# A shifted loop end and idle matrix products in TensorE's waits, in a four-layer convolution network

## The reference, cut to what matters

```python
x = x + _L0_conv_ref(_gn(x), w_real, w_imag, b_real, b_imag)   # 3x3 convolution in the Fourier plane, complex weights
x = x + _L1_conv_ref(_gn(x))                                   # gates: sign of a row's product with the sum of the other half
x = x + _L2_conv_ref(_gn(x), W)                                # 3x3 convolution
x = x + _L3_conv_ref(_gn(x), weight)                           # 3x3 convolution
return x
```

## Time and profile before

| what | value |
|---|---|
| median of 3 runs | 4733.0 us (4728.77 to 9641.31) |
| profiled execution | 4716.25 us |
| its span | 4714.5 us |
| granted TensorE clock, mean over the span | 0.959 |
| busy: TensorE, VectorE, ScalarE | 4226.5, 3331.8, 2541.0 us |

### The profile page before, as it was taken

The page is one execution under the profiler, slowest core; times in us unless marked ns, Lnnn a source line. Parts: engine busy times, 40 slices in busy tenths (PEclk is TensorE's granted clock), DMA queues, the critical chain, the costliest instruction groups (busy, mean ns, idle before and its releaser), DMA issues.

```text
span 4714.5 us, 229091 instructions
## 1 busy us (share of the span) xinstructions
PE 4226.5 (90%) x84848; PEld 2660.6 (56%) x84848; DVE 3331.8 (71%) x13348; ACT 2541.0 (54%) x8637; POOL 1.0 (0%) x6
## 2 busy tenths in 40 slices
PE   4898989989899898998989989899898999988799
PEld 1455765556555566555655556555665556655476
DVE  1887658876588665887658876588756887578873
ACT  4675526655267542775437754377533675335552
POOL 0000000000000000000000000000000000000000
PEclk8999999989999899999999999999999998999999
DMA  7442015520156202661026610356003560034304
GB/s 190 128 136 77 4 40 179 186 82 4 43 184 188 73 4 56 185 187 60 3 66 189 187 46 3 87 184 189 28 3 104 181 185 18 3 99 140 96 4 146
DMA packets 290241, 467.98 MB, mean 99 GB/s; under 512 B 25536, under 2 KB 92288, under 8 KB 289408
## 3 DMA queue, kind: packets, MB, share of 16 engines
q1 hardware_dynamic: 289536, 457.92, 32.2%
HBM read 323.60 MB, written 134.22 MB: 97 GB/s over the span
## 4 chain that ended last, share of the span: by engine, by line
PE 60%; DVE 12%; DMA 8%; issue 8%; SPq 5%; ACT 3%; DVEq 1%; ACTq 1%
PE ps L1352 35%; PE ps L1255 9%; DMA raw<-x 8%; PE ps L1270 4%; PE ps L1263 3%; PE ps L1279 3%; PE ps L1125 2%; DVE shared L858 2%; SPq L426 2%; SPq L433 1%; DVE xin L853 1%; DVE shared L854 1%; ACT x L584 1%; SPq L407 1%; DVE shared L860 1%
## 5 line engine op out<-in xcount | busy, mean ns | idle before, releaser
L1352 PE MATMUL ps<-x,conv_s 32*32 32x512 f32 x49104 | 1753.1, 608 | 76.2 <-DVE x L1016 41.0
L1352 PEld LDWEIGHTS ps<-x,conv_s 32*32 32x32 f32 x49104 | 1246.7, 104 | 520.0 <-issue 290.2
L1255 PE MATMUL ps<-shared 32*32 32x512 f32 x16384 | 654.0, 603 | 0.0
L662 ACT ACTIVATE x<-ps,vec 128x256 f32<-128x256 f32 x512 | 214.6, 470 | 738.6 <-PE ps L1352 738.6
L1270 PEld LDWEIGHTS ps<-hil,shared 128*128 128x128 f32 x4096 | 500.3, 193 | 194.1 <-issue 193.3
L584 ACT ACTIVATE x<-ps,vec 128x128 f32 (+1 forms) x1024 | 376.7, 384 | 430.2 <-PE ps L1270 429.1
L858 DVE SCALAR_TENSOR_TENSOR shared<-xin,trig 128x128 f32<-128x128 f32 x2048 | 530.9, 299 | 106.6 <-DVE shared L854 98.8
L1279 PE MATMUL ps<-eye,vsb 128*128 128x128 f32 x2048 | 369.0, 303 | 222.5 <-DVE vsb L879 127.5
L1270 PE MATMUL ps<-hil,shared 128*128 128x128 f32 x4096 | 567.5, 282 | 0.0
L1086 DVE SCALAR_TENSOR_TENSOR x<-ps,x 128x256 f32<-128x256 f32 x512 | 214.9, 420 | 423.2 <-ACT x L662 422.3
L1255 PEld LDWEIGHTS ps<-shared 32*32 32x32 f32 x16384 | 306.9, 103 | 280.7 <-issue 217.1
(11 more groups left out here) (202 smaller groups left out, 4641.5 us busy)
## 6 DMA issues: line engine op xcount, KB each, us to landing
out<-x SPq DMA_DIRECT2D x512, 256.0 KB
shared<-x SPq DMA_DIRECT2D x448, 256.0 KB
raw<-x SPq DMA_DIRECT2D x256, 256.0 KB
raw<-x SPq DMA_DIRECT2D x512, 128.0 KB
shared<-t_strip SPq DMA_DIRECT2D x512, 96.0 KB, 4.0
x<-x SPq DMA_DIRECT2D x64, 256.0 KB, 7.9
x<-t_proj SPq DMA_DIRECT2D x1, 2048.0 KB, 13.3
trig<-t_trig SPq DMA_DIRECT2D x1, 512.0 KB, 9.9
```

What stands on the lines that cost most here:

```text
L1255: mm = pe.matmul(ps[TM * cg:TM * cg + TM, bank, :], wst[TM * rg:TM * rg + TM, k, v, a, :], of[TM * rg:TM * rg + TM, :], start=(a == AXS), ...
L1352: mm = pe.matmul(halves(ps[TM * cg:TM * cg + TM, banks[k], :]), conv_s[TM * rg:TM * rg + TM, kw, second, :], x1b[TM * rg:TM * rg + TM, of, ...
```

## The change

On TensorE the statistics behind layer 0 become a function of their own, `first_statistics`, and the loop's body is now convolutions of image i, the first layer of image i + 1 and the first statistics of image i + 1; so the branch stands between `prepare_h` and layer 2. A new function `keep_clock(count)` writes count products of the identity (128 by 128 weights) with 512 columns of a table into bank 2, from which nothing is read before it is written anew. Three stand behind `prepare_z`, three behind `prepare_h`, three behind layer 2 (with a wait of their own, for the eviction of the pair that held bank 2) and two behind the third statistics. In the last image there is no `prepare_z` and no `prepare_h`, but the products stand there too. No other engine's code is changed. Nothing in the output depends on the new products.

```diff
-            def convolutions(i, more):
+            def keep_clock(count):
+
+                for _ in range(count):
+                    pe.matmul(ps[:, BY + 2, :], eye[:], trig[:, 0, :], start=True, stop=True)
+
+            def first_statistics(i, more):
 
                 pe.wait_ge(v_part, i + 1)
                 pe.matmul(ps[:, BH, 0:2], partner[:], vec[:, EPS_Q:EPS_Q + 2], start=True, stop=True).then_inc(p_part, 1)
...
                 if more:
                     prepare_z(i + 1)
+                keep_clock(3)
 
                 pe.wait_ge(v_sums2, i + 1)
                 statistics(G_OUT, vec[:, ST:ST + 2], stat[:, 0:2], gsel, P).then_inc(p_stat2, 1)
                 if more:
                     prepare_h(i + 1)
+                keep_clock(3)
+
+            def convolutions(i, more):
 
                 def taps(n, p, banks, outputs, second, kw, done=None):
...
+                pe.wait_ge(evicted, ev(i, 1 + STRIPS - 2 * DEPTH2 + 4))
+                due()
+                keep_clock(3)
                 pe.wait_ge(v_sums3, i * 2 + 2)
                 statistics(G_OUT, vec[:, ST:ST + 2], stat[:, 0:2], gsel, P).then_inc(p_stat3, 1)
+                keep_clock(2)
                 pe.wait_ge(v_conv3, i + 1)
...
             first_layer(0, True)
+            first_statistics(0, True)
             with pe.Fori(0, B - 2) as i:
                 convolutions(i, True)
                 first_layer(i + 1, True)
+                first_statistics(i + 1, True)
             convolutions(B - 2, True)
             first_layer(B - 1, False)
+            first_statistics(B - 1, False)
             convolutions(B - 1, False)
```

## The result

The changed kernel takes 4703.97 us in the median of 17 runs (4688.93 to 4716.78), against 4733.55 us for the kernel before, measured beside it. The ratio is 0.9934, with a 95% interval from 0.9922 to 0.9946: about 30 us faster, as forecast. By parts the fit is looser, as the traces show.

The account below looks back on a forecast made before the run. TensorE, busy 90% of the span, was taken to lose time at the loop's branch and to half clock after idling. Terms −14.2 + 3.5 − 8 − 5 − 6 gave about −30 us, from 4733.0 to 4703 us; range 4670 to 4733.

Parts of the forecast that it names:

- The loop's end: Branch between layer 0 and the partner product: moving it behind prepare_h takes 14.2 us off the path.
- The first group: Three idle products before the second statistics: they delay these by 0.5 us in seven images, +3.5 us in all.
- The second group: Three idle products behind prepare_h: they give back 8 of 30.8 us lost to the clock at layer 2's start.
- Between layer 2 and layer 3: Idle products in the two waits there: faster one-column products save 5 us, bounds 0 and 9.6.
- The start of layer 3: First 6 us of layer 3: a third of the 17.5 us lost to the clock comes back, 6 us.
- the mean clock of layer 2's starts: Sign of being right: granted clock of layer 2's first 14 us above 0.75 on average.
- the hidden branch: Sign of being right: before layer 2, a sequencer branch of 4.6 us that ends before VectorE's gates.
- the 15.5 to 17: Sign of being right: 15.5 to 17 us from layer 0's last product to layer 2 in all images.
- The loop's end alone: Rival: the clock drops all the same and only the moved branch counts, 4725 us; chance 0.24, uncovered branch included.
- the clock held everywhere: Rival: full clock at all starts and one-column products, −72 us, 4661 us; chance 0.14.
- the slower case: Rival: idle products at half clock outlast the waits and become the new wait, +49 us, 4782 us; chance 0.07.
- The uncovered branch: Rival: the moved branch gains nothing before layer 2's dense taps, costing up to 8.5 us; counted within the 0.24.

Follow-up runs that it names:

- the two filled kernels: Two, six, three and three idle products, with the moved loop end (4670.5 us, ratio 0.9855) and with the loop's end where it was (4676.42 us, 0.9886).
- thin: The changed kernel with idle products of one column instead of 512; 4723.74 us, ratio 0.9965 to the kernel before.
- first_only: The changed kernel with only the three products before the second statistics, other groups and the eviction wait removed; 4713.49 us, ratio 0.9963 to before.
- filled: The changed kernel with two, six, three and three idle products instead of three, three, three and two; 4670.5 us, ratio 0.9855 to before.
- loop_only: The changed kernel without any idle products or the wait for evictions, only the moved loop end; 4725.84 us, ratio 0.9989 to before.

## Why the prediction was right, and where only its sum was

*The loop's end (−14.2 us).* Its place on the path was right: 14.9 us less in the stretch with the loop's end alone, 14.0 between the two filled kernels, no "issue" in front of layer 2, and the branch hidden. In whole runs it measured 5 us alone (0.9989, up to 14 by the interval), 17 and 18 in the two other kernels that have the moved end and whose products leave layer 2 starting at half clock (`thin`, `first_only`), and 15 with the filled waits. So 14.2 fits, but how much of it arrives in whole runs is not settled closer than that.

*The first group (+3.5).* 128.7 and 129.2 us stand against 124.2 with the loop's end alone, so +4.5 to +5, and +5.8 where it stands alone. The term fell short by 1 to 2 us; image 0 alone bore 2.2 us (17.8 in place of 15.6), where I had put 0.5 on each image. What I did not see is its second price: the clock that it raises shortens the second group, and opens the idling in which the clock falls.

*The second group (−8).* I named the 2.8 us left idle and took a quarter of the loss as recovered. From before to after the loss fell from 30.8 and 39.7 us to 19.3 and 18.4, and layer 2 as a whole became 16 us shorter (means of two traces each, 877.1 to 861.2). But two traces of one kernel differ there by 9 us. The six traces without full-width products behind `prepare_h` lost 18.9 to 39.2 us, 29.9 in the mean; the three with three in front and three behind lost 20.4 in the mean. By that the second group brought 9.5 us (layer 2 was 9 us shorter), so the term was of the right size or too small by up to 8; the traces can't tell.

*Between layer 2 and layer 3 (−5).* Too small: 82.1 us became 74.6 and 73.7, −8. The one-column stretches took 27.8 us in all before, and 19.0 and 17.9 after. The bias products ran wholly at full clock in three and in four of the eight images (1.4 us) and partly at half in the others (up to 2.1); the first of the one-column products follows 1.3 to 1.5 us of idling. I had kept 5 of 9.6. Over more traces the stretch is 82.8 us in the mean without full-width products in it and 73.1 with three and two, −10.

*The start of layer 3 (−6).* Too large for the changed kernel: 17.5 and 18.8 us lost became 17.1 and 15.1, next to nothing, and layer 3 did not get shorter (984.6 and 988.4 to 988.2 and 985.8). Over more traces it comes nearer: five without full-width products between the layers lost 19.1 us in the mean there, six with three and two 13.7, and their layer 3 was 3.3 us shorter. The prediction had warned that the clock may be down again behind the one-column stretch. With three products in the second wait the loss is 4.9 to 7.9 us.

So by the two kernels' own traces the parts are −10 − 16 − 8 + 0 = −34, and by the means over more traces −10 − 9 − 10 − 3 = −32; the runs say −30. That the sum came out so near is in part luck: a term too small and one too large met in it. The rest of a trace, layer 0, lies between 2194.9 and 2219.0 us over the fourteen traces and moved by 16 us between the two of before, and that is why the first two traces differ by 7 us only. Of the signs that the prediction named, the mean clock of layer 2's starts (0.83) and the hidden branch came as said; image 0's 17.8 us from layer 0 to layer 2 lies outside the 15.5 to 17.

*The rivals.* The loop's end alone falls by `loop_only` and `thin`, whose intervals lie above that of the changed kernel, the clock held everywhere by the windows, the slower case since the kernel got faster: the first group's delay was 5 us and no other group outlasted its wait. The uncovered branch is refuted by the row of L1458.

## What to carry to other kernels

Fill a wait up to the start of the dense work, not from its beginning, and count the length of idle products at the clock that they will run at: here three that ended 2.8 us ahead of layer 2 left 18 to 19 us lost over eight starts, and six that ended 0.3 us ahead at most (`filled`) left none. Taking products away made this kernel faster by 22 us, since in most images those left then ran at half clock to the end of the wait. Where a gain is 0.6% and one stretch moves by 16 us between two executions of the same kernel, sum the stretches that the change touches and leave the total to the runs.

## What the runs showed that was not expected

The branch back of the image loop takes 3.3 to 3.9 us where layer 2 follows it, over all traces, against 3.8 to 4.8 where the statistics follow; the exit takes 0.08 us in both. Dense taps behind a taken branch did not stall: with the wait filled, layer 2 began 0.23 to 0.30 us late for "issue" in images 1 to 5, and by as much (0.23) in image 0, where no branch is taken.

The length of the idling does not decide a start alone. With full-width products behind `prepare_h`, all 39 starts with at most 1.7 us of idling lost 0.1 us or less. Of 22 with 2.7 to 2.8 us, three lost nothing, 13 lost 1.4 to 1.7 and six 5.1. In the 21 of these with a first group of three, 5.1 were lost in just those six in which the first group took 3.12 us or longer, and at most 1.7 where it took 3.08 or less. Why is open.

The one-column products of the bias (48 instructions) take 1.39 us at full clock and 2.16 at half, so the clock is worth a third and not half there.
